# Second cross attention: exponentials straight from the score bank, and the gated projection added on VectorE

## What is computed

```
def _L1_xattn_ref(x, y, wq, bq, wk, bk, wv, bv, wo, bo):    # 16 heads of 32, 120 keys a batch
    q = (x @ wq + bq).reshape(B, SQ, N_HEADS, D_HEAD)
    k = (y @ wk + bk).reshape(B, SKV, N_HEADS, D_HEAD)
    v = (y @ wv + bv).reshape(B, SKV, N_HEADS, D_HEAD)
    scores = jnp.einsum('bqhd,bkhd->bhqk', q, k) / jnp.sqrt(D_HEAD)
    attn = jax.nn.softmax(scores, axis=-1)
    out = jnp.einsum('bhqk,bkhd->bqhd', attn, v).reshape(B, SQ, D_EMBED)
    return out @ wo + bo
...
x = x + jnp.tanh(g_xattn[1]) * _L1_xattn_ref(_layernorm(x), ctx_768, ...)
```

## Time and profile before

| | before |
|---|---|
| median of 3 runs | 4028.98 us (4025.55 to 4050.93) |
| profiled execution | 4035.9 us, span 4034.1 us |
| TensorE busy in the span | 3717.7 us (92%) |
| VectorE | 2914.3 us (72%) |
| ScalarE | 1904.2 us (47%) |
| GpSimd | 1063.2 us (26%) |
| bodies 0 to 7 of `attention1` | 2095 to 2560 us |

### The profile page before, as it was taken

The page is one execution under the profiler, slowest core; times in us unless marked ns, Lnnn a source line. Parts: engine busy times, 40 slices in busy tenths (PEclk is TensorE's granted clock), DMA queues, the critical chain, the costliest instruction groups (busy, mean ns, idle before and its releaser), DMA issues. The chain is left out here.

```text
span 4034.1 us, 62650 instructions
## 1 busy us (share of the span) xinstructions
PE 3717.7 (92%) x21848; PEld 2940.4 (73%) x21848; DVE 2914.3 (72%) x4500; ACT 1904.2 (47%) x2703; POOL 1063.2 (26%) x990
## 2 busy tenths in 40 slices
PE   7899999999789999999958999759999999999998
PEld 4555666556478898989935555459988898889897
DVE  5576766666668787877627887577887777777785
ACT  2555655555445555554415445214444444444443
POOL 2222221122011111111035654213233323333331
PEclk9999999999899999999979999769999999999999
DMA  4100000000167777776431221137777767776774
GB/s 157 31 29 18 26 31 32 31 26 9 71 228 247 275 252 265 265 248 208 161 113 42 85 76 49 44 104 222 218 224 227 230 202 220 226 227 207 216 237 124
DMA packets 386020, 595.28 MB, mean 148 GB/s; under 512 B 26127, under 2 KB 192079, under 8 KB 385551
## 3 DMA queue, kind: packets, MB, share of 16 engines
q1 hardware_dynamic: 352575, 521.68, 38.6%
q0 software_dynamic: 23856, 56.15, 6.3%
q10 hardware_dynamic: 9368, 14.33, 1.0%
HBM read 532.96 MB, written 59.12 MB: 147 GB/s over the span
## 5 line engine op out<-in xcount | busy, mean ns | idle before, releaser
L1409 PE MATMUL bank<-e_xh,e_WH 128*128 128x256 f32 x1984 | 572.3, 288 | 38.8 <-issue 32.6
L1250 DVE TENSOR_TENSOR e_all<-e_all_raw,e_WH 128x2048 fp32r<-128x2048 f32 x240 | 547.3, 2289 | 67.8 <-ACT e_WH L1244 67.1
L1409 PE MATMUL bank<-e_xl,e_WH 128*128 128x256 f32 x1984 | 570.4, 288 | 0.0
L1409 PE MATMUL bank<-e_xh,e_all 128*128 128x256 f32 x1984 | 570.1, 287 | 0.0
L1244 ACT ACTIVATE e_WH<-e_all_raw 128x2048 fp32r<-128x2048 f32 x240 | 458.3, 1910 | 221.7 <-DMA e_all_raw<-in_w 221.7
L1462 PE MATMUL bank<-e_WH,e_hh 128*128 128x512 f32 x1192 | 474.2, 398 | 0.0
L1462 PE MATMUL bank<-e_WH,e_hl 128*128 128x512 f32 x1192 | 468.3, 393 | 0.0
L1409 PEld LDWEIGHTS bank<-e_xh,e_WH 128*128 128x128 f32 x1984 | 387.7, 195 | 44.0 <-issue 42.1
L1409 PEld LDWEIGHTS bank<-e_xl,e_WH 128*128 128x128 f32 x1984 | 387.7, 195 | 0.9
L1409 PEld LDWEIGHTS bank<-e_xh,e_all 128*128 128x128 f32 x1984 | 387.3, 195 | 0.0
L1485 ACT ACTIVATE e_sil<-bank 128x256 f32<-128x256 f32 x248 | 95.3, 384 | 398.9 <-PE bank L1409 398.9
(11 more groups left out here) (380 smaller groups left out, 9206.2 us busy)
## 6 DMA issues: line engine op xcount, KB each, us to landing
e_all_raw<-in_w SPq DMA_DIRECT2D x320, 512.0 KB, 4.6
f_wl_raw<-in_w SPq DMA_DIRECT2D x120, 1024.0 KB, 5.6
e_all_raw<-in_w SPq DMA_DIRECT2D x80, 1024.0 KB, 5.3
e_rest_raw<-in_w SPq DMA_DIRECT2D x72, 1024.0 KB, 5.5
f_X<-in_x SPq DMA_DIRECT2D x32, 256.0 KB, 2.7
f_R<-in_x SPq DMA_DIRECT2D x32, 256.0 KB, 4.4
x<-f_R SPq DMA_DIRECT2D x32, 256.0 KB, 2.0
a_X<-x SPq DMA_DIRECT2D x32, 256.0 KB, 3.4
```

The costliest lines, as they stand in the source:

```text
L1250: dve.tensor_tensor(self.WL(p), self.raw(p), self.WH(p).bitcast(F32), ALU.subtract).then_inc(self.w_ready.sem, 1)
L1409: mm = nc.tensor.matmul(up[n % RING][:, q * ROWS:q * ROWS + ROWS], w, xx[:, c, :], start=(c == 0 and i == 0), stop=(c == DC - 1 and i == 2))
```

## The change

For each head ScalarE now reads the scores from the bank and writes the exponential to `Pr`, with minus the scaled maximum as the bias: eight instructions of 120 columns for one of 960. VectorE makes these biases (`nmax`, 128x8) and no longer writes the difference of 960 columns. The pair of score banks is free after the exponentials, and TensorE waits for `exp_done` instead of `centred`. `gated` and ScalarE's part for o are gone: VectorE's `result` computes bank times gate plus X in one instruction and by that empties the bank; SP waits for the same.

```diff
@@ SP
-                            sp.wait_ge(x3_ready, QT * (n - 1) + t + 1)
+                            wait_emptied(sp, n - 1, ("o", t))
@@ TensorE, scores
                     if u >= 2:
-                        pe.wait_ge(centred, u - 1)
+                        pe.wait_ge(exp_done, u - 1)
@@ ScalarE
                 def exp(u):
-                    act.wait_ge(centred, u + 1)
-                    act.activation(Pr[:, u % 3, :, :, :], Pr[:, u % 3, :, :, :], ACT.Exp, scale=DH1 ** -0.5).then_inc(exp_done, 1)
+                    act.wait_ge(nmax_done, u + 1)
+                    if u >= 3:
+                        act.wait_ge(turned[1], u - 2)
+                    for h in range(2):
+                        for g in range(4):
+                            x = act.activation(Pr[:, u % 3, h, g, :], Sb[u % 2][:, h, g, :], ACT.Exp,
+                                               bias=nmax[:, u % 3, 4 * h + g:4 * h + g + 1], scale=DH1 ** -0.5)
+                    x.then_inc(exp_done, 1)
...
-                    if kind == "r" or not there(n, f):
+                    if kind in ("o", "r") or not there(n, f):
...
-                    elif kind == "o":
-                        if QT * i + a >= 2:
-                            act.wait_ge(x3_ready, QT * i + a - 1)
-                        x = act.activation(gated[:, a % 2, :], m, ACT.Copy, scale=k.gate[:, 1:2])
@@ VectorE
-                def centre(u):
+                def largest(u):
                     flat8 = smax[:, u % 3, :].rearrange("p (h g) -> p h g", h=2)
                     dve.wait_ge(s_done, u + 1)
                     dve.tensor_reduce(flat8, Sb[u % 2], AX.X, ALU.max).then_inc(max_done, 1)
                     dve.wait_ge(max_done, u + 1)
-                    if u >= 3:
-                        dve.wait_ge(turned[1], u - 2)
-                    dve.tensor_tensor(Pr[:, u % 3, :, :, :], Sb[u % 2], flat8.unsqueeze(3).to_broadcast([P, 2, 4, CL]), ALU.subtract)\
-                        .then_inc(centred, 1)
+                    dve.tensor_scalar(nmax[:, u % 3, :], smax[:, u % 3, :], -DH1 ** -0.5, None, ALU.mult).then_inc(nmax_done, 1)
...
                     a, x = QT * i + t + 1, X[:, i % 4, t, :]
+                    bk_, c_ = fill(i, f)
+                    dve.wait_ge(filled[bk_], c_)
+                    dve.wait_ge(r_biased, a)
+                    dve.scalar_tensor_tensor(x, mb[bk_], k.gate[:, 1:2], x, ALU.mult, ALU.add).then_inc(emptied[bk_], 1)
                     wait_emptied(dve, i, f)
-                    dve.wait_ge(r_biased, a)
-                    dve.tensor_tensor(x, x, gated[:, t % 2, :], ALU.add).then_inc(x3_ready, 1)
-                    dve.wait_ge(x3_ready, a)
```

More of the change, by code:

```diff
@@ L1657, in attention1 @@
         smax, ssum, rinv = sb("smax", [P, 3, HS]), sb("ssum", [P, 3, HS]), sb("rinv", [P, 3, HS])
+        nmax = sb("nmax", [P, 3, HS])
         PT = sb("PT", [P, 2, HS, S])
         OT, N3, N3T = sb("OT", [P, DC, S]), sb("N3", [P, 2, D]), sb("N3T", [P, 2, DC, P])
-        gated = sb("gated", [P, 2, D])
         bank = k.bank
@@ L1673, in attention1 @@
         bn3_step, stat3, veps3_step, rst3, n3_ready = (sem(n) for n in ("bn3_step", "stat3", "veps3_step", "rst3", "n3_ready"))
-        r_biased, x3_ready = sem("r_biased"), sem("x3_ready")
+        r_biased = sem("r_biased")
         filled, emptied = [sem(f"filled{i}") for i in range(2)], [sem(f"emptied{i}") for i in range(2)]
         turned, pt_out = [sem(f"turned{i}") for i in range(2)], [sem(f"pt_out{i}") for i in range(2)]
-        s_done, max_done, centred, exp_done = sem("s_done"), sem("max_done"), sem("centred"), sem("exp_done")
+        s_done, max_done, nmax_done, exp_done = sem("s_done"), sem("max_done"), sem("nmax_done"), sem("exp_done")
         sum_done, rinv_done, p_ready = sem("sum_done"), sem("rinv_done"), sem("p_ready")
@@ L2034, in _ @@
                         if softmax(n):
-                            centre(u)
+                            largest(u)
                         if s in NORM3_AT and 0 <= n - 1 < B:
```

## The result

| | before | after |
|---|---|---|
| median on the same chip | 4032.55 us (6 runs, 4025.55 to 4050.93) | 4051.77 us (6 runs, 4044.45 to 4060.37) |
| ratio of the times | | 1.0047, 95% interval 1.0025 to 1.0069 |
| profiled execution, span | 4035.9, 4034.1 us | 4053.35, 4051.6 us |
| VectorE, ScalarE busy in the span | 2914.3, 1904.2 us | 2843.7, 1953.5 us |

The change makes the kernel about 19 us slower (10 to 28 us by the interval). 4051.77 lies within the range of 4014 to 4058, in the upper part of it that was there for the rivals 2 and 4. The sum had said 5 us: its direction was right and its size was not. Two runs of the kernel before among those beside the experiments, 4290.05 and 13648.39 us at a lower clock, are left out of every comparison.

What follows compares the result with a forecast made beforehand. The prediction took TensorE to bound the kernel, with its waits and clock the only gains. Its terms, -5.2 + 4.5 + 4.4 + 2.5 - 1, summed to +5.2 us, giving 4034 us, range 4014 to 4058.

Steps and rivals of the forecast that it cites:

- rival 2: TensorE's clock falls behind r 0 in all seven bodies and sometimes in step 2: 4044 to 4050 us, chance 0.14.
- r 0 behind step 4, bodies 2 to 5: TensorE's r 0 in step 6 starts earlier, gaining 1.3 us in each of these bodies, together 5.2.
- A 128x8 instruction, 0.20 like the reciprocal on the same shape: VectorE's new instruction making the biases (L1995) takes 0.20 us.
- The max-to-max sum of 6.58 us and r 0 at 20.0: VectorE needs 6.58 us between maxima in steps 4 to 6; r 0 starts about 20.0 us after step 4 starts.
- The exponentials, 2.2 us: On ScalarE, eight overlapping exponentials take 2.2 us in place of one of 1.00.
- The addition at 0.75, never stalled: VectorE's addition reading the bank (L2010) takes 0.75 us throughout, without the old stall of 4.18.
- Rivals 3 and 4: Exponentials do not overlap: 4075 us, chance 0.05; GpSimd holds up the addition from the bank: 4060 us, chance 0.05.
- Step 2, wait 1.87: TensorE's wait of 1.14 us, with yt 1 behind the exponentials, grows by 0.73: +4.4 us in six bodies.
- The clock behind r 0, four of seven at 3.2 us each: TensorE's clock falls in about four of seven bodies: 0 us, with -12.8 and +9.6 as ends.
- VectorE and ScalarE together now set the pace: In steps 4 to 6 their 6.58 us exceeds TensorE's work of about 5.5 and 5.9 us.
- rival 5: VectorE leaves the path and nothing replaces it; four waits of 3.94 and the clock are won: 4001 us, chance 0.04.
- The end, -1: Body 8 has only the o chains, about 0.6 us less each, part of it hidden: -1 us.

Runs made afterwards that it cites:

- e1: Kernel after, with the eight maxima written to unused columns of the score bank, so the 128x8 instruction reads PSUM: 4038.94 us, ratio 1.0031.
- e3: Kernel before with only the change's addition from the bank, without `gated`: 4017.56 us, ratio 0.9978.
- e4: Kernel after, with yt 1 emptied ahead of the exponentials in step 2: 4050.54 us, ratio 1.0052.
- e7: Kernel before with the addition from the bank, o 3's addition ahead of the sums, and yt 1 copied before the exponential in step 2: 3995.69 us.
- e2: Kernel before with the eight exponentials from the bank alone, `gated` and the SBUF addition kept: 4056.32 us, ratio 1.0066.
- e6: Kernel before with the addition from the bank, and o 3's addition ahead of the sums in step 6: 4003.36 us, ratio 0.9944.
- e8: Kernel after without the 128x8 instruction (maxima negated in the reduction), o 3's addition ahead of the sums, yt 1 first: 4000.88 us.
- e5: Kernel after, with o 3's addition ahead of the sums in step 6: 4037.77 us, ratio 1.0028.
- e9: Kernel before with the addition from the bank, yt 1 copied first, and o 3's addition in front of `norm3` in step 6: 3989.26 us, ratio 0.9894.

## Why the forecast was right in direction and short in size

The steps of the forecast, in us, from the starts of `scores` in the profiled executions, each against before. e1 stands beside it, since it is the kernel that the forecast had in mind:

| term | forecast | after | e1 |
|---|---|---|---|
| r 0 behind step 4, bodies 2 to 5 | -5.2 | -0.8 | -5.3 |
| the same, bodies 1 and 6 | +4.5 | +8.2 | +3.9 |
| body 7, to its step 7 | 0 | +5.1 | +1.3 |
| step 2, bodies 1 to 6 | +4.4 | +4.9 | +5.0 |
| step 3, bodies 1 to 6 | 0 | +6.2 | +6.1 |
| from r 0 to the next body (clock), bodies 1 to 6 | 0 | -2.9 | +0.1 |
| body 0 | +2.5 | +3.8 | +2.3 |
| steps 0 and 1, bodies 1 to 6 | 0 | +0.9 | -1.6 |
| sum to step 7 of body 7 | +6.2 | +25.4 | +11.7 |
| from there to the last logits | -1 | -9.4 | -8.5 |

The distance of 18 us between 4034 and 4051.77 has two parts. 3.6 us are the base: the forecast stood on 4028.98 for the kernel before, the median of 3 runs, which by 6 runs is 4032.55. The other 14 are the terms above with the last stretch.

**"A 128x8 instruction, 0.20 like the reciprocal on the same shape": this step failed.** It takes up to 1.25 us, in 21 of 64 over 0.3. It was put at the price of the nearest shape, and the right neighbour was the nearest kind. The kernel before had it: its tensor_scalar from SBUF to SBUF, L1985, in the stage (min, median, max):

```profile
L1985 DVE TENSOR_SCALAR a_Y<-a_X,a_mv,a_rstd x32: 516/539/1480, 2050.9 to 2470.1; 128x512 f32<-128x512 f32 x32
```

A maximum of 1480 ns beside a median of 539 says that this kind is held up too. In the three first rows of the table and in body 0 the difference between after and e1 is 4.5 + 4.3 + 3.8 + 1.5 = 14.1 us. e1 removed nothing but the stall; that the whole 14.1 is its price is an estimate from two executions, in which the clock differs as well. The times show 8 to 13 us. The prediction used the rule of the Trainium skill on ports (SBUF — State Buffer) for the addition alone. The same page, section "Who interferes with whom", names tensor_scalar among the operations that can take the pair of ports shared with GpSimd, and says that whoever is first has it for the whole instruction. The rows agree: 1.25 us beside L1755 and 0.17 without, 0.165 to 0.168 in all 64 where the input is PSUM. They add that eight columns are enough for it.

**The max-to-max sum of 6.58 us and r 0 at 20.0: right for the kernel without the stall.** e1 has 19.93 to 20.03 in the bodies 2 to 5. In the bodies 1 and 6, with 19.70, the loss was right too.

**The exponentials, 2.2 us: right** (2.12). One alone takes 0.378, so the next starts (2.12 - 0.378) / 7 = 0.25 us after the last; the forecast had 0.354 and 0.254. The rule of the Trainium skill (ScalarE: Activation LUTs, "What ACT_TABLE_LOAD costs") has the single one right, 0.380 us. Its overlap of 93 ns is too small for this run of eight, where 0.129 are measured, and the 2.39 us estimated from it are too long.

**The addition at 0.75, never stalled: right** (708 to 752 ns, and e3 the same). Rivals 3 and 4 are out.

**Step 2, wait 1.87: right** (1.78). **That nothing follows from it was wrong.** Rival 2 mentioned it, the sum left it out. Granted clock behind this wait (third column from the end), in body 2 and in body 3 of the kernel after:

```profile
2229.00:2233.00 4.00, 3.86 (x20) 3.04 (x21) 2.07 (x5) 1.83 (x4) 2.54 (x3) 0.64 0.00 0
2295.00:2299.00 4.00, 3.93 (x27) 2.96 (x28) 2.22 (x5) 2.83 (x8) 2.56 (x3) 1.00 0.00 0
```

TensorE stood 1.78 us ahead of each. In body 2 it then had the lower level of 1.2 GHz for a part of the stretch and in body 3 not; where it has, step 3 takes 10.7 to 11.0 us instead of 9.34, in four bodies of six. The four times 1.6 are the 6.2 us of the table. e4 and e7, which have no wait there, have no such step.

**The clock behind r 0, four of seven at 3.2 us each: a guess, and that the term of 0 came out near is luck.** In the kernel after step 7 is long in five of the bodies 1 to 6, with waits of 2.97, 3.25 and 1.89 us, and the clock falls behind r 0 of body 7 too: six of seven, nearly what rival 2 had. But each of the five costs 1.6 to 1.7 us (11.81 to 11.87 against 10.18 from r 0 to the next body) and not 3.2. Before, the four cost 2.3 to 3.3, together 11.2 and not 12.8, since body 3 had been taken for all. More falls at a lower price make the -2.9 of the table, where rival 2 had +9.6. With its falls in step 2 rival 2 comes nearest to the measured time (4044 to 4050), but one of its two terms is not there, and the stall of L1995 is in no rival. What decides on a fall is open. In e1 the same wait ends in body 3 with a fall and in body 4 without:

```profile
2319.50 1.87 PE L1879 MATMUL bank<-a_gw,a_N3T 128*128 128x8 f32 x8 [2.12 <-DVE a_X L2011]
...
2384.55 1.06 PE L1879 MATMUL bank<-a_gw,a_N3T 128*128 128x8 f32 x8 [2.12 <-DVE a_X L2011]
```

Eight matmuls in 1.87 us and the same eight in 1.06. Shorter waits do not keep the clock up either: in e2 it falls behind 0.91 us at r 0, and in e6, e7 and e8 behind 1.07 to 1.10 in two of four bodies each. The bodies 2 and 3 of e6 about their r 0 (2247.25 and 2307.15), which waited 1.09 and 1.08 us:

```profile
2248.00:2252.00 4.00, 4.00 (x17) 2.76 (x17) 3.36 (x6) 0.60 (x1) 3.96 (x4) 0.57 0.94 285
2306.00:2312.00 6.00, 4.92 (x27) 3.29 (x27) 5.47 (x9) 1.64 (x4) 5.41 (x7) 1.00 0.65 189
```

The prediction's reading of the earlier trace rows, a fall behind 3.00 us and none behind 1.70, gives no border between them. So the clock can't be forecast from the length of the wait between 0.9 and 2.2 us; it needs a range.

**"VectorE and ScalarE together now set the pace": right**, and this is why rival 5 (4001 us) did not come true; only e8, with three more edits, gets there. One thing stood in its way that the forecast had named and not priced as an option: that VectorE frees the bank of o 3 behind the sums. e5 and e6 show what it is worth, 14 us each (4051.77 to 4037.77, 4017.56 to 4003.36, medians of different chips in both cases); taken against the kernel before on its own chip it is 10 and 14.

**Busy times.** ScalarE's about 35 us of a body was right (34.4), VectorE's below 38 too low (41.2), since in these 58 us L1995 takes 3.2 us and `norm3` (L2022) 4.1 where 1.4 and 2.5 were to be expected at 0.20 and at the length of before. `share` lost its long cases, as forecast (at most 1800 ns).

**The end, -1: not testable.** The last stretch, 50 us from 40 us behind the start of body 7, before and after:

```profile
2550.10:2600.10 50.00, 41.40 (x172) 24.64 (x170) 19.34 (x36) 14.81 (x24) 12.05 (x17) 0.78 0.17 64
```

```profile
2570.21:2620.21 50.00, 41.13 (x192) 24.36 (x192) 21.20 (x41) 15.66 (x37) 12.49 (x17) 0.89 0.17 63
```

The clock was 0.78 before and 0.89 after. From the start of body 7 to the last logits the twelve profiled executions of this case take 84.0 to 100.2 us, e6 the least and e4 the most. The 9.4 us that the profiled pair shows here are at least in part the clock of one execution, and this is why the spans differ by 17.5 us where the stage was 25 behind.

## What to carry to other kernels

Price a small new instruction by its kind and its operands' memories, not by its shape: look in the trace for the same operation with the same sources and destination, and at its maximum, not at its median. On VectorE, a tensor_scalar from SBUF to SBUF, or an addition of two operands in SBUF, that stands at the head of a chain while GpSimd works may take GpSimd's time instead of its own; let it read PSUM, or fold it into the instruction ahead of it. Not all that reads SBUF is held up: the sums (L1999), the statistics (L2012) and the reciprocals (L2002) stay at 1.15, 0.70 and 0.21 us at most, also where they start under GpSimd. And where an engine takes over the freeing of a buffer, put that work in front of what nobody waits for: here the exchanged instruction brought 11 us (e3), and the changes of order on top of it 34 more (e9).

## What the runs showed of the hardware that was not expected

- A tensor_scalar of 128x8 from SBUF to SBUF takes 0.171 us alone and up to 1.253 beside a GpSimd addition; with its input in PSUM 0.165 to 0.168 in 64 of 64, 26 of them under GpSimd (e1).
- An addition with both inputs in SBUF stood 4.07 us (e2) and 4.18 while GpSimd worked, until 0.56 us behind the end of its two back-to-back instructions of 1.28 and 1.80. It did so though it had started 0.60 us ahead of the first of them (2303.13 against 2303.73); GpSimd was then in an indirect DMA (L1763, 2302.76 to 2303.71), so that who came first is not settled. An addition with an input in PSUM never took over 0.752 (64 in two kernels).
- Eight exponentials of 120 columns with a per-partition bias start every 0.25 us, though one takes 0.38.
- Behind waits of 1.1, 1.78 and 2.12 us TensorE's clock was at 1.2 GHz in some bodies and at 2.4 in others with the same instructions around them. A fall costs 1.3 to 1.6 us in step 3 and 1.6 to 3.7 behind r 0; behind the waits of 1.1 that is more than the wait itself.
